# Causal mask of the row maxima: from a matmul per unit to VectorE's reducing instruction

## What is computed

```python
scores = jnp.einsum('bhqd,bhkd->bhqk', q, kh) / jnp.sqrt(jnp.float32(D))
scores = jnp.where(allowed_pos[None, None], scores, NEG)
causal = jnp.triu(jnp.ones((S, S), bool), k=1)
scores = jnp.where(causal[None, None], -jnp.inf, scores)
p = jax.nn.softmax(scores, axis=-1)
out = jnp.einsum('bhqk,bhkd->bhqd', p, vh)
```

## Time and profile before

| what | value |
|---|---|
| median of 3 runs | 3361.42 us (3355.58 to 3364.91) |
| the profiled execution, its own time | 3359.99 us |
| its span in the profile | 3358.2 us (1.8 us lie around it) |
| busy over the span: PE, PEld, DVE, ACT, POOL | 92%, 60%, 52%, 37%, 58% |
| mean granted TensorE clock | 0.957 of full speed |
| self attention in steady state, one group | 42.5 us |
| natural scores' mask matmuls (line 1086) | 512, 231 ns each in the profile |
| maxima of self attention on DVE (line 976) | 512, 752 ns each |

### The profile page before, as it was taken

The page is one execution under the profiler, slowest core; times in us unless marked ns, Lnnn a source line. Parts: engine busy times, 40 slices in busy tenths (PEclk is TensorE's granted clock), DMA queues, the critical chain, the costliest instruction groups (busy, mean ns, idle before and its releaser), DMA issues. The chain is left out here.

```text
span 3358.2 us, 41317 instructions
## 1 busy us (share of the span) xinstructions
PE 3106.1 (92%) x16138; PEld 2029.5 (60%) x16138; DVE 1762.3 (52%) x2373; ACT 1226.5 (37%) x2305; POOL 1942.2 (58%) x896
## 2 busy tenths in 40 slices
PE   7978997999999995987999999999967999999999
PEld 6867885455555543863444444444426888888887
DVE  4526554666666654776777777777713221222221
ACT  2112220455555552220656566666652211111111
POOL 3214333577777776652888888888877533334332
PEclk9988997899999997995999999999988999999999
DMA  6535545544444404545324242424014100110100
GB/s 207 176 121 180 182 164 161 105 102 102 102 102 102 102 14 147 199 158 143 72 55 98 55 98 51 99 54 98 11 52 131 38 26 26 38 38 26 38 13 13
DMA packets 198545, 310.30 MB, mean 92 GB/s; under 512 B 15544, under 2 KB 91832, under 8 KB 198352
## 3 DMA queue, kind: packets, MB, share of 16 engines
q1 hardware_dynamic: 198352, 307.68, 33.2%
HBM read 189.04 MB, written 117.44 MB: 91 GB/s over the span
## 5 line engine op out<-in xcount | busy, mean ns | idle before, releaser
L941 POOL TENSOR_TENSOR e_probs<-e_probs 128x2048 f32<-128x2048 f32 x160 | 733.0, 4583 | 175.9 <-ACT e_probs L1050 171.1
L1050 ACT ACTIVATE e_probs<-e_st 128x512 f32<-128x512 f32 x1024 | 554.4, 598 | 406.2 <-PE e_st L1104 396.4
L976 DVE TENSOR_REDUCE e_neg_max<-e_nat 128x1 f32<-128x1024 f32 x512 | 602.3, 1218 | 148.4 <-PE e_nat L1082 143.5
L941 POOL TENSOR_TENSOR b_probs<-b_probs 128x1536 f32<-128x1536 f32 (+1 forms) x144 | 446.7, 3102 | 224.9 <-ACT b_probs L1050 215.1
L1050 ACT ACTIVATE b_probs<-b_st 128x512 f32<-128x512 f32 (+3 forms) x768 | 350.5, 490 | 386.8 <-PE b_st L1108 298.9
L976 DVE TENSOR_REDUCE b_neg_max<-b_nat 128x1 f32<-128x128 f32 (+7 forms) x512 | 365.0, 752 | 181.5 <-PE b_nat L1086 179.0
L1402 POOL TENSOR_TENSOR m_hid_lo<-m_hid,m_hid_hi 128x512 fp32r<-128x512 f32 x128 | 168.3, 1315 | 390.3 <-DVE m_hid_hi L1439 390.3
L1104 PE MATMUL e_st<-e_qs,e_ks 99*128 99x512 f32 x1024 | 387.4, 429 | 4.3 <-ACT e_probs L1050 2.9
L1082 PE MATMUL e_nat<-e_ks,e_qs 96*128 96x512 f32 x1024 | 343.4, 425 | 40.9 <-DVE e_neg_max L976 28.0
L1439 DVE CAST m_hid_hi<-m_hid 128x512 fp32r<-128x512 f32 x128 | 58.9, 460 | 570.1 <-ACT m_hid L1318 570.1
L1104 PEld LDWEIGHTS e_st<-e_qs,e_ks 99*128 99x128 f32 x1024 | 174.4, 189 | 257.7 <-ACT e_probs L1050 199.8
(11 more groups left out here) (197 smaller groups left out, 5284.3 us busy)
## 6 DMA issues: line engine op xcount, KB each, us to landing
b_qs<-sq_hi SPq DMA_DIRECT2D x30, 512.0 KB, 6.7
b_ks<-sk_hi SPq DMA_DIRECT2D x30, 512.0 KB, 14.4
e_qs<-cq_hi SPq DMA_DIRECT2D x30, 512.0 KB, 6.9
e_ks<-ck_hi SPq DMA_DIRECT2D x30, 512.0 KB, 14.8
d_x<-in_ctx SPq DMA_DIRECT2D x8, 1024.0 KB, 6.1
ck_hi<-d_part_hi SPq DMA_DIRECT2D x32, 256.0 KB, 6.1
ck_lo<-d_part_lo SPq DMA_DIRECT2D x32, 256.0 KB, 6.0
cv<-d_tok_out SPq DMA_DIRECT2D x32, 256.0 KB, 4.8
```

What stands on the lines that cost most here:

```text
L941: pool.tensor_tensor(into, into, probs[:, home(n, k), :, first:TOK], ALU.add).then_inc(added, 1)
L976: dve.tensor_reduce(neg_max[:, u:u + 1], nat[:, bank_of[u]:bank_of[u] + banks, 0:keys // banks], AX.XY, ALU.max, negate=True).then_inc(max ...
L1050: act.activation(probs[:, home(n, k), j, first:TOK], st_ps[:, bank_at("scores", blk), first:TOK], ACT.Exp).then_inc(exped, 1)
```

## The change

The mask matmul of the natural scores goes. `mask_qk` grows from 128 to 1024 columns, 0 in the first 896 and the triangle in the last 128, so that its last `keys` columns are the mask of any unit. For the causal stage DVE's reduction is replaced by `tensor_tensor_reduce`: it reads the unit's scores from PSUM and the mask from SBUF, writes -(score + mask) back over the scores in PSUM, and keeps the minimum, which is the negated maximum. Cross attention keeps the old reduction.

```diff
+                    found = nat[:, bank_of[u]:bank_of[u] + banks, 0:keys // banks]
+                    if causal:
+                        masked = mask_qk[:, S - keys:S].rearrange("p (b t) -> p b t", b=banks)
+                        dve.tensor_tensor_reduce(out=found, in0=found, in1=masked, scale=-1.0, scalar=3.0e38, op0=ALU.add,
+                                                 op1=ALU.min, accum_out=neg_max[:, u:u + 1]).then_inc(maxed, 1)
+                    else:
+                        dve.tensor_reduce(neg_max[:, u:u + 1], found, AX.XY, ALU.max, negate=True).then_inc(maxed, 1)
...
-                        diagonal = causal and bank == banks - 1
                         last = pe.matmul(nat[:, bank_of[u] + bank, 0:cols], qs[p][0:rows, j, t * P:(t + 1) * P],
-                                         ks[p][0:rows, j, bank * width:bank * width + cols], start=True,
-                                         stop=not diagonal)
-                        if diagonal:
-                            last = pe.matmul(nat[:, bank_of[u] + bank, width - P:width], ident_bf[:], mask_qk[:],
-                                             start=False, stop=True)
+                                         ks[p][0:rows, j, bank * width:bank * width + cols], start=True, stop=True)
...
-        mask_qk, mask_kq = sb("mask_qk", [P, P], BF16), sb("mask_kq", [P, P], BF16)
+        mask_qk, mask_kq = sb("mask_qk", [P, S], BF16), sb("mask_kq", [P, P], BF16)
...
-                    pool.affine_select(out=t[:], in_=t[:], compare_op=op, fill=fill, base=0,
+                    pool.affine_select(out=t[:, -P:], in_=t[:, -P:], compare_op=op, fill=fill, base=0,
```

More of the change, by code:

```diff
@@ L975, in maximum @@
                         dve.wait_ge(max_turned, n)
-                    dve.tensor_reduce(neg_max[:, u:u + 1], nat[:, bank_of[u]:bank_of[u] + banks, 0:keys // banks], AX.XY,
-                                      ALU.max, negate=True).then_inc(maxed, 1)
+                    found = nat[:, bank_of[u]:bank_of[u] + banks, 0:keys // banks]
[5 more added lines that the diff above has]
+                        dve.tensor_reduce(neg_max[:, u:u + 1], found, AX.XY, ALU.max, negate=True).then_inc(maxed, 1)
                 def split_max(n):
```

## The result

The changed kernel takes 3323.2 us (median of 5, 3321.4 to 3326.4) against 3356.7 us for the kernel before, measured beside it (median of 5, 3355.5 to 3364.9). The ratio is 0.9895 with a 95% interval of 0.9881 to 0.9908: 33 us faster, by more than a measurement is uncertain. The forecast was 3321 us.

The account below looks back on a forecast made before the run. PE was taken to bound a group, with waits for DVE. Four stretches save 2.65 us of 42.5; over fifteen groups 39.8, less 0.7 at the start, 39 us off 3359.99: 3321 us, range 3308 to 3366.

Parts of the forecast that it names:

- The mask matmul, 0.125 us from start to start: PE, natural scores: removing one mask matmul saves 0.125 us; 32 in a group make 4.0 us if PE were never held.
- Readiness 0.07 earlier: Natural scores: a unit becomes ready for DVE 0.07 us earlier, so each place hanging on readiness gains 0.055 less.
- a second pass: Rival, DVE's maxima: writing over scores in PSUM costs 2.08 ns for each key, about 3523 us; chance 0.11.
- The cuts: PE's path in a group, split where another engine or a DMA holds it: 2.65 us less of 42.5.
- Terms 3 and 4: Turn to first turned score, 0.42 us gained, capped by the maxima rows' DMA; then to the waiting 1024-key unit, 0.10.
- Term 2: From the 768-key neighbour's wait to the turn of the maxima: seven masks, 0.41 us gained together.
- Term 1: From the 1024-key unit to the next that waits for its 768-key neighbour: 15 masks count, 1.72 us gained.
- The head: Group 0's 32 units at half clock: later maxima balance saved masks, zero gain, with 2 us to each side.
- The fill at the start: POOL fills 896 more mask columns ahead of everything, uncovered: 0.7 us added.
- Fifteen groups: Self attention: fifteen groups run beside natural scores, the last has none; the gain over them is 39.8 us.
- DVE takes back: Rival: 0.35 us or more extra per unit on DVE leaves 0.6 us gain a group, 3351 us; chance 0.15.
- the masks were hidden anyway: Rival: ACT's exponentials or POOL's sums would hold PE instead, gain under 10 us; chance 0.04.

Follow-up runs that it names:

- second profile: The changed kernel run once more, instruction for instruction (only a product's factors swapped): 3322.1 us, ratio 0.9876.
- the early high row: Kernel without any mask on the maxima, with SP sending the high row of the maxima once split off, not awaiting the low one: 3313.8 us, ratio 0.9870.

## Why the prediction was right

The time was 3323.2 us for a forecast of 3321, in a range of 3308 to 3366. That the two lie 2 us apart is in part luck. The forecast took 39 us off an execution of 3360.0; measured are 33.5 us off a median of 3356.7. The gain was 5.5 us too large, and the start was 3.3 too high. By its steps:

- **The mask matmul, 0.125 us from start to start: right.** 0.13 for each of four put back on PE's own stretch.
- **Readiness 0.07 earlier: right.** In the same burst the first maximum starts 0.55 us behind its unit's first matmul (870.69 to 871.24) where it was 0.63 (920.73 to 921.36): 0.08.
- **The main instruction costs what a reduction does: nearly.** 36 ns more at 1024 keys on average: 8 ns for a unit by itself, which the write to PSUM explains, and some 50 for one that starts along with a write-out, whose cause is open. The rival of a second pass falls: 1254 ns where it needed some 2200.
- **The write-out: the delay right, the occupancy wrong.** I took 0.10 us of delay to PE's signal. From the start of the maximum to the turn it was 1.27 us (934.61 to 935.88) and is 1.35 (843.87 to 845.22): 0.07 to 0.08. But I had the write-out end the overlap and take 0.16 us of each unit, 33.0 us of DVE in a group. Busy time rose by 1.5 us, 0.05 a unit, since the next main instruction starts along with the write-out. From start to start it is 0.01 for the first pair of a run and 0.05 for one behind another.
- **The cuts: right as a mechanism.** Terms 3 and 4 came within 0.02. Term 2 gained 0.10 more, mostly because the occupancy was 0.05 and not 0.16. Term 1 gained 0.28 less, because of a wait that I had only named as possible: in the run of five units after 867.27 the fifth needs the bank of the second, whose maximum is not yet found (its write-out ends at 868.34). Three matmuls that need 0.235 + 0.15 + 0.15 us by their starts elsewhere take 0.87 from 867.92 to 868.79. Without the pair they take 0.75 (898.23 to 898.98 in the run without masks), so most of this wait comes from the missing mask matmuls, and 0.12 from the pair. Two errors of opposite sign made the sum better than its parts. A slip besides: one mask and not two lies beside the wait that ends term 1. It carried no weight, as the 15 before it were counted right.
- **The head: the balance was wrong, and it did not matter.** From the first natural score to the turn the head went from 29.5 us (562.4 to 592.0) to 27.7, where I had taken zero. But PE then waited 4.16 us for the DMA of the key mask (1.99 before), and 4.63 in the second profile. The DMA sets the end of the head, and the gain stays in that wait.
- **The fill at the start, 0.7 us:** the fill took 0.96 us for 0.20, and the first transfer of the context, which waits for it, left 0.62 us later (3.88 against 3.26). Nothing of it can be told in the time.
- **Fifteen groups:** in its second profile the 14 steps between turns after the first group are 40.05 to 40.83 us, and 15 times 2.47 is 37 us; measured are 33 and, beside the second profile, some 42, which lie around it; the kernel before itself scatters from 3353 to 3371 us over the runs of this study.
- **The rivals.** DVE takes back some of the gain, but only a part of it: 0.44 us a group. PE waits 18 us longer for DVE at the natural scores of the whole stage, but 12 of them without the pair too. The sign that I had set for this wait, 10 to 15 us, was missed for that reason: it left out what a shorter program of PE's does to it. That the masks were hidden anyway falls with 39.66 us in the run without them.

The rule of the Trainium skill weighed in the prediction ("VectorE: DVE Perf Modes", section "Rules for kernel authors": the count of operations is what to keep small) would have the second operation cost DVE a start and a drain of its own. The trace disagrees in size: the 512 write-outs, 141 ns each in their rows, cost DVE's pace 0.01 us from start to start behind the first pair of a run (0.88 against 0.87 at 768 keys) and 0.05 behind another (1.05 against 1.00 at 896). The section "The DRAIN you can't avoid" of the same page of the Trainium skill, from which the prediction took that an operation starts only when the pipe is empty, itself makes an exception for a next operation that is "not held". The old reductions agree with the exception: 0.87 us from start to start for a row of 0.96. The prediction's 60 ns for a write-out, an estimate from the table in the same page's section "The TRN2 errata" of the Trainium skill, lie below both measured rows, 83 and 141 ns.

## What to carry to other kernels

Price an instruction by what it moves from start to start, then cut the bounding engine's program at every place where another engine or a DMA holds it: what is removed before a cut counts in full, what is removed beside the wait counts nothing, and what is late next caps the rest. An operation that serves only a bound can sometimes be dropped: leaving the mask off the maxima was faster than either way of adding it (39.66 us a group against 40.10 and 42.57). The softmax takes any bound that is not so far above the largest allowed score that all its exponentials vanish; whether that holds depends on the data. When a predicted total comes out right, compare it term by term all the same; here a new wait, a smaller occupancy and a high starting point hid one another.

## What was not expected of the hardware

The instruction that writes out the accumulated value runs beside the next instruction: its row has 141 ns, yet the next main instruction starts with it, and is then some 34 ns longer than one that starts alone (1267 against 1233 ns at 1024 keys). The write-out's duration follows the target of the main instruction before it, 141 ns after a write of fp32 to PSUM and 83 ns after one of bytes to SBUF.

The granted clock, at half in the stage's head, rose to full at different times in like programs: between 605 and 610 us in the kernel before, from 610 to 615 in a second execution of the changed kernel, at 625 in the first and in the run that writes to SBUF, with no wait of PE's over 0.1 us in the profile between 602 and 625 of the first. Its first group was 5.6 us longer than in the second execution; no run isolates the half clock as the cause, but the profiles of the nearly alike programs fall in line. Where it lasted 14 us into the first group, the group took 42.8 us (the run with four matmuls on PE's own stretch); with 22 us, 46.9 (the early high row); with 29, 48.2 (the output in SBUF); with 31, 50.4 (the first profile).
